# Gate logits with the gate's weights stationary, then turned back, in a post-layernorm attention and mixture-of-experts kernel

## The chip, the cores and the metric

The kernel runs on one core of one Trainium2 chip. The metric is the device time of one execution in microseconds (us). TensorE (PE in the profile) multiplies, ScalarE (ACT), VectorE (DVE) and GpSimd (POOL) do the rest of the arithmetic, and SyncE (SP) starts most of the transfers.

## What is computed

The reference is one transformer layer on x of shape (2, 2048, 256), all in fp32:

```
x = layernorm(x + attention(x))            # 16 heads of 16, rotary, causal
tokens = x.reshape(4096, 256)
logits = tokens @ gate_w.T                 # 8 experts
probs = softmax(logits); expert = argmax(probs)
rank = position of the token among its expert's tokens; kept if rank < 640
y = probs[expert] * (relu(token @ w1[expert] + b1) @ w2[expert] + b2)
x = layernorm(x + y)
```

The change touches the line with the logits alone.

## The kernel before, in words

The program has four stages, one after the other: `project_qkv`, `attention`, `project_and_gate` and `experts`. Each is a block in which every engine has its own instruction list, and the engines meet at semaphores. A stage ends when all its engines have ended, since the next takes over the memory.

`project_and_gate` (from L774) handles the 4096 tokens in eight chunks of 512; a chunk is four tiles of 128 tokens. On PE, the order is written out by hand in `both(n, ...)` (L994 to L1012), which holds the second half of chunk n and the gate of chunk n - 1:

- `turn_o` (L931, matmuls at L937) turns the attention output of a tile so that tokens lie on the partitions. DVE's `normalise` (L1100, L1102) divides by the softmax denominators.
- `turn_y` (L941, L947) turns the result back, ACT's `copy_yT` (L1039) copies it out of PSUM, and `project` (L952, L958) multiplies it by the output weights. DVE's `residual` (L1111, L1114, L1118) adds x and takes the statistics.
- `turn_x1` (L962, L966) turns a chunk's normalised rows (DVE's `norm_chunk`, L1123 to L1134) into psD, and ACT's `copy_x1T` (L1050) copies them to x1T: 256 channels in two halves (kt = 0, 1) on the partitions, 512 tokens along the free axis.
- `gate_logits` (L970, L976) multiplies x1T by the gate's weights: for each of four tiles and two halves, the 128 x 128 block of x1T is the stationary operand and the 8 columns of the weights are streamed. The result, 128 tokens x 8 experts for each tile, is in `logits`, a part of the bank psL.
- DVE's `choose` (L1154 to L1163) reads it: maximum, difference, one-hot choice. ACT's `exponentials` (L1054) needs the difference; PE's `rank_chunk` (L984 to L991) needs the one-hot; DVE's `place` (L1168 to L1190) needs both and gives each token its slot. POOL's `send` (L1245) scatters the rows to DRAM by the slots.

The order on DVE (`both`, L1192 to L1206) is fixed too: rest of normalise and residual 0 to 2 of chunk n, `choose(n - 1)`, residual 3, normalise 0 and 1 of chunk n + 1, `place(n - 1)`, `norm_chunk(n)`. ACT's (`both`, L1065 to L1074) is: copy_yT 0, two plain_rows (L1062, the rows with the second normalisation applied, stored to the output), copy_yT 1, two more, copy_yT 2, copy_x1T(n - 1), copy_yT 3, exponentials(n - 1), and `deviations(n)` with two square roots, L1043 and L1045. Exp and Sqrt need different function tables, so each chunk has two table loads.

After the eighth chunk the lists end with its gate alone: on PE `turn_x1`, `gate_logits`, `rank_chunk` (L1028 to L1030), on ACT `copy_x1T`, four `plain_rows`, `exponentials` (L1083 to L1085), on DVE `choose` and `place`, on POOL the last sends.

A matmul with fp32 operands stands in the trace as two records; a transpose as one. So L976 has 8 chunks x 4 tiles x 2 halves x 2 = 128 records.

Of the kernel before, what the change touches and what calls it, by code (L numbers as in the profile page):

```python
# [30 lines left out]
P = 128  # L31
B, T, C, H = 2, 2048, 256, 16
HS = C // H
KT = C // P
E, DFF = 8, 1024
CAP = math.ceil(1.25 * B * T / E)
CHUNK = 512
# [736 lines left out]
def project_and_gate(nc, x, o_d, wproj, bproj, gate, ident, before, ones, prefer, slot_base, tok0, slots_d, out_d,  # L774
# [4 lines left out]
    with ExitStack() as ctx:  # L779
        def sb(name, shape, dt=F32):  # L780
            return ctx.enter_context(nc.sbuf_tensor(name, shape, dt))
# [4 lines left out]
        def sem(name):  # L786
            return ctx.enter_context(nc.semaphore(name))
# [28 lines left out]
        rows = [sb(f"rows{i}", [P, TPC, RW]) for i in range(2)]  # L816
        plain = [sb(f"plain{i}", [P, TPC, C]) for i in range(2)]
        x1T = sb("x1T", [P, KT, CHUNK])
        top = sb("top", [P, TPC])
        shifted = sb("shifted", [P, TPC, E])  # L820
        wanted = sb("wanted", [P, TPC, E])
# [42 lines left out]
        plain_stored = [sem(f"plain_stored{i}") for i in range(2)]  # L864
        x1_turned = sem("x1_turned")
        x1T_ready = sem("x1T_ready")
        logits_ready = sem("logits_ready")
        gate_step = sem("gate_step")
        shifted_ready = sem("shifted_ready")
# [56 lines left out]
        @block.tensor  # L926
        def _(pe):
            pe.wait_ge(w_loaded, 16 * (n_w - 1))

            def turn_o(n, i, h, t):  # L930
                if t == 0:  # L931
                    pe.wait_ge(loaded[i], 32 * (h + 1))
                if not (isinstance(n, int) and n == 0 and t < 2):

                    pe.wait_ge(y_ready, 1 + TPC * n + t - 1)
                for g in range(NG):
                    last = nc.tensor.transpose(psA[t % 2][:, g * P:(g + 1) * P], o_s[i][:, g, t * P:(t + 1) * P],  # L937
                                               id_s[:])
                last.then_inc(o_turned, 1)

            def turn_y(n, t):  # L941
                m = TPC * n + t
                pe.wait_ge(y_ready, 1 + m + 1)

                pe.wait_ge(yT_ready, 1 + m)
                for kt in range(KT):
                    last = nc.tensor.transpose(psB[:, kt, :],  # L947
                                               y_s[t % 2][:].rearrange("p h d -> p (h d)")[:, kt * P:(kt + 1) * P],
                                               id_s[:])
                last.then_inc(y_turned, 1)  # L950

            def project(n, t):  # L952
                m = TPC * n + t
                pe.wait_ge(yT_ready, 1 + m + 1)

                pe.wait_ge(res_ready, 1 + m)
                for kt in range(KT):
                    last = nc.tensor.matmul(psC[t % 2][:, 0:C], yT[t % 2][:, kt, :], wproj_s[:, kt, :],  # L958
                                            start=(kt == 0), stop=(kt == KT - 1))
                last.then_inc(projected, 1)  # L960

            def turn_x1(n, i):  # L962
                pe.wait_ge(rows_ready, TPC * (n + 1))
                for kt in range(KT):
                    for t in range(TPC):
                        last = nc.tensor.transpose(psD[:, kt, t * P:(t + 1) * P],  # L966
                                                   rows[i][:, t, kt * P:(kt + 1) * P], id_s[:])
                last.then_inc(x1_turned, 1)

            def gate_logits(n):  # L970
                pe.wait_ge(x1T_ready, KT * (n + 1))

                pe.wait_ge(slots_ready, 1 + n)
                for t in range(TPC):
                    for kt in range(KT):
                        last = nc.tensor.matmul(logits[:, t, :], x1T[:, kt, t * P:(t + 1) * P], gate_s[:, kt, :],  # L976
                                                start=(kt == 0), stop=(kt == KT - 1))
                last.then_inc(logits_ready, 1)

            def rank_chunk(n):  # L980


                pe.wait_ge(onehot_ready, n + 1)
                nc.tensor.matmul(ranks[:], before_s[:], onehot[:], start=True, stop=False)  # L984
                for t in range(TPC - 1):
                    later = TPC - 1 - t
                    nc.tensor.matmul(ranks[:, t + 1:TPC, :], ones_s[:],
                                     onehot[:, t:t + 1, :].to_broadcast([P, later, E]),
                                     start=False, stop=(t == TPC - 2))
                for t in range(TPC):  # L990
                    last = nc.tensor.matmul(counts, ones_s[:], onehot[:, t, :], start=(t == 0), stop=(t == TPC - 1))  # L991
                last.then_inc(ranks_ready, 1)

            def both(n, i, h, h_next):  # L994


                turn_y(n, 0)
                turn_o(n, i, h, 2)
                turn_y(n, 1)
                project(n, 0)  # L1000
                turn_o(n, i, h, 3)
                turn_y(n, 2)
                project(n, 1)
                turn_x1(n - 1, 1 - i)
                turn_y(n, 3)
                project(n, 2)
                gate_logits(n - 1)
                project(n, 3)
                if h_next is not None:
                    turn_o(n + 1, 1 - i, h_next, 0)  # L1010
                    turn_o(n + 1, 1 - i, h_next, 1)
                rank_chunk(n - 1)  # L1012

            turn_o(0, 0, 0, 0)
            for t in range(TPC):
                if t + 1 < TPC:
                    turn_o(0, 0, 0, t + 1)
                turn_y(0, t)
                if t:
                    project(0, t - 1)  # L1020
            project(0, TPC - 1)
            turn_o(1, 1, 0, 0)
            turn_o(1, 1, 0, 1)
            for k in range(0, NC3 // 2 - 1):
                both(2 * k + 1, 1, k, k + 1)
                both(2 * k + 2, 0, k + 1, k + 1)
            both(NC3 - 1, 1, NC3 // 2 - 1, None)
            turn_x1(NC3 - 1, 1)  # L1028
            gate_logits(NC3 - 1)
            rank_chunk(NC3 - 1)  # L1030

        @block.scalar
        def _(act):
            act.wait_ge(w_loaded, 16 * (n_w - 1))
            act.wait_ge(set_up, 2)

            def copy_yT(n, t):
                act.wait_ge(y_turned, TPC * n + t + 1)
                nc.scalar.activation(yT[t % 2][:], psB[:], ACT.Copy).then_inc(yT_ready, 1)  # L1039

            def deviations(n, i):
                act.wait_ge(mv_ready, TPC * (n + 1))
                nc.scalar.activation(std[i][:], mv[i][:, :, 1], ACT.Sqrt, bias=eps_s[:]).then_inc(std_ready, 1)  # L1043
                act.wait_ge(var_step, 2 * (n + 1))
                nc.scalar.activation(std2[i][:], var2[i][:], ACT.Sqrt, bias=eps_s[:]).then_inc(std2_ready, 1)  # L1045

            def copy_x1T(n):
                act.wait_ge(x1_turned, n + 1)
                for kt in range(KT):
                    nc.scalar.activation(x1T[:, kt, :], psD[:, kt, :], ACT.Copy).then_inc(x1T_ready, 1)  # L1050

            def exponentials(n):
                act.wait_ge(shifted_ready, n + 1)
                nc.scalar.activation(expd[:], shifted[:], ACT.Exp).then_inc(exp_ready, 1)  # L1054

            def plain_rows(n, i, h, tiles):

                if tiles[0] == 0:
                    act.wait_ge(rstd2_ready, n + 1)
                    act.wait_ge(plain_stored[i], 1 + 16 * h)  # L1060
                for t in tiles:
                    nc.scalar.activation(plain[i][:, t, :], rows[i][:, t, 0:C], ACT.Copy,  # L1062
                                         scale=rstd2[i][:, t:t + 1]).then_inc(plain_ready, 1)

            def both(n, i, h_before):  # L1065
                copy_yT(n, 0)
                plain_rows(n - 1, 1 - i, h_before, (0, 1))
                copy_yT(n, 1)
                plain_rows(n - 1, 1 - i, h_before, (2, 3))
                copy_yT(n, 2)  # L1070
                copy_x1T(n - 1)
                copy_yT(n, 3)
                exponentials(n - 1)
                deviations(n, i)  # L1074

            for t in range(TPC):
                copy_yT(0, t)
            deviations(0, 0)
            for k in range(0, NC3 // 2 - 1):
                both(2 * k + 1, 1, k)  # L1080
                both(2 * k + 2, 0, k)
            both(NC3 - 1, 1, NC3 // 2 - 1)
            copy_x1T(NC3 - 1)  # L1083
            plain_rows(NC3 - 1, 1, NC3 // 2 - 1, range(TPC))
            exponentials(NC3 - 1)  # L1085

# [600 lines left out]
```

## Time and profile before

| what | us |
|---|---|
| median of 3 runs (lowest, highest) | 1468.92 (1464.8, 1473.62) |
| the profiled execution's own time | 1471.45 |
| its span, first to last instruction | 1469.4 |
| `project_and_gate` in the span, about | 1064 to 1205 |
| mean granted TensorE clock over the span | 0.928 |

Positions are microseconds from the start of the span. A busy time is that of an engine; idle time stands in square brackets in a timeline, with what ended it. A granted clock of 1.00 is 2.4 GHz and 0.50 is 1.2 GHz.

### The profile page before, as it was taken

Reading aid. Unit: us, or ns where it says so; the run is one execution under the profiler, and the core shown is the slowest. Engines: PE = TensorE matmul, PEld = TensorE weight load, DVE = VectorE, ACT = ScalarE, POOL = GpSimd, SP = SyncE. Lnnn points to the kernel's source line nnn. Section 1 sums busy time; section 2 is a strip of 40 time slices with the busy share of each in tenths; the row PEclk is TensorE's granted clock in tenths of the full one; section 3 lists DMA queues with packets and bytes.
Section 4 is the critical chain, followed back from the end, with each engine's and each line's share of the span. In section 5 each row is a group of like instructions: output and inputs, shape, how many; then the busy total and the mean of one; then the engine's idle time right before and its main releaser. Section 6 shows DMA issues by size and latency. Waiting matters only on the chain. (4 is left out here: it accounts for less than half of the span.)

```text
span 1469.4 us, 22852 instructions
## 1 busy us (share of the span) xinstructions
PE 1285.6 (87%) x7857; PEld 650.4 (44%) x7857; DVE 1197.5 (81%) x2812; ACT 798.6 (54%) x1130; POOL 277.3 (19%) x282
## 2 busy tenths in 40 slices
PE   6776379999999999999999999999577739999997
PEld 3433112333333333333333333332166638999997
DVE  5997679999999989999999999994067737888886
ACT  3443303666666666666666666667535434554542
POOL 3555430011010010110010110101233420211121
PEclk9888656999999999999999999999888859999998
DMA  4578454213113112121130130000346531334230
GB/s 147 162 213 255 144 123 74 67 35 87 31 30 87 31 53 63 31 82 35 50 96 26 35 88 9 8 16 9 109 135 196 170 106 66 122 98 152 94 98 24
DMA packets 119120, 126.90 MB, mean 86 GB/s; under 512 B 15452, under 2 KB 101599, under 8 KB 119008
## 3 DMA queue, kind: packets, MB, share of 16 engines
q1 hardware_dynamic: 115424, 117.00, 27.5%
q0 software_dynamic: 3584, 8.47, 1.6%
q8 instruction: 63, 1.03, 0.3%
q14 instruction: 49, 0.40, 0.1%
HBM read 83.02 MB, written 48.38 MB: 89 GB/s over the span
## 5 line engine op out<-in xcount | busy, mean ns | idle before, releaser
L656 ACT ACTIVATE probs<-scores 128x1024 f32<-128x1024 f32 (+3 forms) x640 | 539.0, 894 | 320.4 <-PE scores L549 319.6
L711 DVE TENSOR_REDUCE part_max<-ring 128x1 f32<-128x512 f32 x768 | 478.0, 683 | 24.7 <-PE ring L579 23.1
L579 PE MATMUL ring<-k_stack,q_stack 96*128 96x512 bf16 (+3 forms) x1280 | 406.6, 363 | 45.0 <-DMA k_stack<-pieces_d 30.0
L549 PE MATMUL scores<-q_stack,k_stack 99*128 99x512 bf16 (+3 forms) x1280 | 339.3, 349 | 2.4 <-ACT probs L656 1.6
L565 PE MATMUL out_p<-probs,v_s 128*32 128x512 f32 (+3 forms) x2560 | 299.8, 540 | 0.5 <-POOL probs L761 0.3
L579 PEld LDWEIGHTS ring<-k_stack,q_stack 96*128 96x128 bf16 x1280 | 114.9, 97 | 350.3 <-DVE part_max L711 147.7
L761 POOL TENSOR_SCALAR_AFFINE_SELECT probs<-probs 128x512 f32<-128x512 f32 x128 | 81.4, 636 | 773.4 <-ACT probs L656 773.4
L705 DVE CUSTOM_DVE_ANT_0 scratch<-ring,mask_s 128x384 f32<-128x384 f32 (+2 forms) x384 | 195.0, 550 | 17.2 <-issue 16.5
L549 PEld LDWEIGHTS scores<-q_stack,k_stack 99*128 99x128 bf16 x1280 | 112.8, 98 | 175.7 <-issue 65.2
L195 PE MATMUL psP<-xT,wqk_s 128*128 128x512 f32 x128 | 72.2, 728 | 35.4 <-ACT xT L234 30.9
L1425 PE MATMUL psY<-w_hi,h_hi 128*128 128x256 f32 x320 | 91.0, 284 | 0.0
L1427 PE MATMUL psY<-w_hi,h_lo 128*128 128x256 f32 x320 | 89.8, 281 | 0.0
L1426 PE MATMUL psY<-w_lo,h_hi 128*128 128x256 f32 x320 | 89.8, 281 | 0.0
L1459 ACT ACTIVATE h_whole<-psH,b_s 128x384 f32<-128x384 f32 (+1 forms) x128 | 66.9, 528 | 41.0 <-PE psH L1406 34.2
L565 PEld LDWEIGHTS out_p<-probs,v_s 128*32 128x32 f32 x2560 | 50.6, 107 | 87.3 <-issue 58.2
L1404 PE MATMUL psH<-x_hi,w_hi 128*128 128x384 f32 (+1 forms) x256 | 80.2, 313 | 7.9 <-issue 6.8
L1590 POOL DMA_INDIRECT out<-fin,token x40 | 44.6, 1114 | 212.8 <-DVE fin L1543 206.8
L1405 PE MATMUL psH<-x_lo,w_hi 128*128 128x384 f32 (+1 forms) x256 | 79.5, 311 | 0.0
L1406 PE MATMUL psH<-x_hi,w_lo 128*128 128x384 f32 (+1 forms) x256 | 79.4, 310 | 0.0
L195 PEld LDWEIGHTS psP<-xT,wqk_s 128*128 128x128 f32 x128 | 29.3, 235 | 74.7 <-issue 41.4
L1467 ACT ACTIVATE w_hi<-w_whole 128x1024 fp32r<-128x1024 f32 x32 | 33.5, 1057 | 51.8 <-DMA w_whole<-w 39.0
L1425 PEld LDWEIGHTS psY<-w_hi,h_hi 128*128 128x128 f32 x320 | 60.9, 190 | 0.0
(116 smaller groups left out, 1498.4 us busy)
## 6 DMA issues: line engine op xcount, KB each, us to landing
w_whole<-w SPq DMA_DIRECT2D x16, 1024.0 KB, 6.5
q_stack<-pieces_d SPq DMA_DIRECT2D x192, 64.0 KB, 2.9
k_stack<-pieces_d SPq DMA_DIRECT2D x192, 64.0 KB, 2.9
v_d<-vt SPq DMA_DIRECT2D x8, 1024.0 KB, 4.4
v_s<-v_d SPq DMA_DIRECT2D x8, 1024.0 KB, 6.1
o_d<-o_s SPq DMA_DIRECT2D x32, 256.0 KB, 2.2
p_o<-o_d SPq DMA_DIRECT2D x8, 1024.0 KB, 6.1
slots_d<-no_row SPq DMA_DIRECT2D x1, 5200.0 KB, 30.0
```

Source lines behind the costliest of these rows:

```text
L195: last = nc.tensor.matmul(psP[:, g, :], wqk_s[:, kt, g * P:(g + 1) * P], xT[i][:, kt, :], start=(kt == 0), stop=(kt == KT - 1))
L549: last = nc.tensor.matmul(scores[p][:, hh, off:CHUNK], k_stack[i][0:KROWS, kb // TPC, j, kb % TPC * P:(kb % TPC + 1) * P], q_stack[i][0:KR ...
L565: last = nc.tensor.matmul(out_p[j * VW:(j + 1) * VW, off:CHUNK], v_s[i][:, kb, j * VW:(j + 1) * VW], probs[n % NPROB][:, j, off:CHUNK], st ...
L579: last = nc.tensor.matmul(slot[:, h * w:(h + 1) * w], q_stack[i][0:SROWS, qt // TPC, j + h, qt % TPC * P:(qt % TPC + 1) * P], k_stack[i][0 ...
L656: nc.scalar.activation(probs[n % NPROB][:, 2 * p:2 * p + 2, off:CHUNK], scores[p][:, :, off:CHUNK], ACT.Exp, scale=SCALE).then_inc(exp_don ...
L705: nc.vector.tensor_tensor_reduce(out=scratch[:, j, 0:w], in0=ring[m % 3][:, 0:w], in1=mask_s[:, CHUNK - w:CHUNK], scale=1.0, scalar=LOWEST ...
L711: nc.vector.tensor_reduce(part_max[:, qt, j, t:t + 1], ring[m % 3][:, 0:w], axis=AX.X, op=ALU.max).then_inc(ring_read, 1)
L761: nc.gpsimd.affine_select(out=block_, in_=block_, compare_op=ALU.is_ge, fill=0.0, base=0, pattern=[[0, HPU], [1, P]], channel_multiplier=- ...
L1404: nc.tensor.matmul(out, w_hi[i][0][:, kt, cols], hi, start=(kt == 0), stop=False)
L1425: nc.tensor.matmul(out, h_hi[:, ft, slots], w_hi[i][1][:, ft, :], start=(ft == 0), stop=False)
L1426: nc.tensor.matmul(out, h_hi[:, ft, slots], w_lo[i][1][:, ft, :], start=False, stop=False)
L1427: last = nc.tensor.matmul(out, h_lo[:, ft, slots], w_hi[i][1][:, ft, :], start=False, stop=(ft == FT - 1))
```

## The change

The product is formed the other way round: `gate_logits` now streams the 512 tokens of x1T against the gate's 8 columns as the stationary operand, one matmul for each half, into 8 partitions of psD (free, since x1T was copied out of it). ACT copies the 8 x 512 result to a new tile, `gated_s`, in `copy_gated`. A new function on PE, `turn_logits`, turns it tile by tile into the old place in psL. On PE `turn_logits(n - 1)` stands after `project(n, 3)`; on ACT `copy_gated(n - 1)` stands after the fourth copy_yT and ahead of the exponentials. After the eighth chunk `copy_gated` stands ahead of the four plain_rows. The wait for `slots_ready` moves to `turn_logits`. DVE, POOL and SP are as before.

```diff
             def gate_logits(n):
                 pe.wait_ge(x1T_ready, KT * (n + 1))
+                for kt in range(KT):
+                    last = nc.tensor.matmul(psD[0:E, 0, :], gate_s[:, kt, :], x1T[:, kt, :],
+                                            start=(kt == 0), stop=(kt == KT - 1))
+                last.then_inc(gated, 1)
+
+            def turn_logits(n):
+                pe.wait_ge(gated_copied, n + 1)
 
                 pe.wait_ge(slots_ready, 1 + n)
                 for t in range(TPC):
-                    for kt in range(KT):
-                        last = nc.tensor.matmul(logits[:, t, :], x1T[:, kt, t * P:(t + 1) * P], gate_s[:, kt, :],
-                                                start=(kt == 0), stop=(kt == KT - 1))
+                    last = nc.tensor.transpose(logits[:, t, :], gated_s[:, t * P:(t + 1) * P], id_s[0:E, 0:E])
                 last.then_inc(logits_ready, 1)
...
                 gate_logits(n - 1)
                 project(n, 3)
+                turn_logits(n - 1)
...
             gate_logits(NC3 - 1)
+            turn_logits(NC3 - 1)
             rank_chunk(NC3 - 1)
...
+            def copy_gated(n):
+                act.wait_ge(gated, n + 1)
+                nc.scalar.activation(gated_s[:], psD[0:E, 0, :], ACT.Copy).then_inc(gated_copied, 1)
...
                 copy_yT(n, 3)
+                copy_gated(n - 1)
                 exponentials(n - 1)
...
             copy_x1T(NC3 - 1)
+            copy_gated(NC3 - 1)
             plain_rows(NC3 - 1, 1, NC3 // 2 - 1, range(TPC))
             exponentials(NC3 - 1)
```

## Rows read from the trace of the kernel before

**Rows 1.** Busy time by engine in the stage `project_and_gate`.
```profile
1064.00:1205.00 141.00, 97.62 (x576) 82.42 (x576) 87.25 (x368) 59.26 (x120) 50.36 (x40) 0.78 0.46 150
```
**Rows 2.** Timeline of a middle chunk: start us, us, engine, line, operation [idle before].
```profile
1101.43 1.08 ACT L1050 ACTIVATE x1T<-psD 128x512 f32<-128x512 f32 x2 [1.60 <-PE psD L966]
1102.57 1.95 PE L976 MATMUL psL<-gate_s,x1T 128*128 128x8 f32 x16 [0.18 <-ACT x1T L1050]
1102.81 1.28 ACT L1054 ACT_TABLE_LOAD   x1
1104.37 1.11 PE L958 MATMUL psC<-wproj_s,yT 128*128 128x256 f32 x4
1104.55 0.19 DVE L1154 TENSOR_REDUCE top<-psL 128x4 f32<-128x32 f32 x1 [0.96 <-PE psL L976]
1105.00 0.23 ACT L1054 ACTIVATE expd<-shifted 128x32 f32<-128x32 f32 x1 [0.91 <-DVE shifted L1156]
1105.32 1.04 PE L937 MATMUL psA<-p_id,p_o 128*128 128x128 f32 x8
1106.75 0.30 ACT L1043 ACTIVATE std<-mv,eps_s 128x4 f32<-128x4 f32 x1 [0.22 <-DVE mv L1118]
1109.33 0.18 DVE L1123 RECIPROCAL rstd<-std 128x4 f32<-128x4 f32 x1
1109.93 0.30 ACT L1045 ACTIVATE std<-var,eps_s 128x4 f32<-128x4 f32 x1 [2.88 <-DVE var L1128]
1110.14 0.36 ACT L1039 ACTIVATE yT<-psB 128x256 f32<-128x256 f32 x1
1110.65 0.66 PE L947 MATMUL psB<-p_id,y_s 128*128 128x128 f32 x2 [2.40 <-ACT yT L1039]
1118.43 1.95 PE L976 MATMUL psL<-gate_s,x1T 128*128 128x8 f32 x16
```
**Rows 3.** Last 2.4 us before each of PE's seven restarts: stretch, PE busy, clock, DMA.
```profile
1077.84:1080.24 2.40, 0.00 (x0) 0.76 0.00 0
1093.55:1095.95 2.40, 0.01 (x1) 1.00 0.00 0
1108.25:1110.65 2.40, 0.00 (x1) 0.83 0.01 3
1124.11:1126.51 2.40, 0.01 (x1) 1.00 0.00 0
1138.72:1141.12 2.40, 0.00 (x1) 0.88 0.00 0
1153.29:1155.69 2.40, 0.00 (x1) 0.69 1.05 360
1168.83:1171.23 2.40, 0.01 (x2) 1.00 0.00 0
```
**Rows 4.** The same view from restart to gate, second and third time.
```profile
1096.00:1102.60 6.60, 6.42 (x31) 0.74 0.46 137
1110.70:1118.40 7.70, 7.64 (x30) 0.61 0.55 145
```
**Rows 5.** Timeline after the eighth chunk.
```profile
1188.31 1.69 ACT L1062 ACTIVATE plain<-rows,rstd 128x256 f32<-128x256 f32 x4
1188.47 3.58 PE L976 MATMUL psL<-gate_s,x1T 128*128 128x8 f32 x16 [1.17 <-ACT x1T L1050]
1192.09 0.19 DVE L1154 TENSOR_REDUCE top<-psL 128x4 f32<-128x32 f32 x1 [6.73 <-PE psL L976]
1193.32 0.18 DVE L1170 TENSOR_REDUCE total<-expd 128x4 f32<-128x32 f32 x1
1195.67 0.97 POOL L1245 DMA_INDIRECT slots_d<-rows,slot_index  x1 [6.68 <-DVE slot_index L1190]
```
**Rows 6.** 512-column fp32 products of the first stage: timeline, then one line's durations.
```profile
55.92 3.60 PE L195 MATMUL psP<-xT,wqk_s 128*128 128x512 f32 x8
L195 PE MATMUL psP<-xT,wqk_s x128: 592/592/1222, 12.3 to 158.2; 128*128 128x512 f32 x128
```

More of the change, by code:

```diff
@@ L818, in project_and_gate @@
         x1T = sb("x1T", [P, KT, CHUNK])
+        gated_s = sb("gated_s", [E, CHUNK])
         top = sb("top", [P, TPC])
@@ L866, in project_and_gate @@
         x1T_ready = sem("x1T_ready")
+        gated = sem("gated")
+        gated_copied = sem("gated_copied")
         logits_ready = sem("logits_ready")
```

## The prediction

> **What bounds the kernel now.** First the busy times of the stage that the change touches [rows 1]: of 141 us PE works 97.62, DVE 87.25, ACT 59.26, POOL 50.36, at a mean clock of 0.78. No engine fills the stage, so it runs on a loop of hand-overs, and the timeline of one chunk shows which. I read it from one gate to the next [rows 2]. G is the start of the gate's products, 1102.57. They end at G+1.95; DVE, which had been idle for 0.96, starts `choose` at G+1.98 and from there works without a gap through residual 3, two normalises and `place` to `norm_chunk` (G+6.76) and its two small products. ACT's second square root waited 2.88 for them (G+7.36), and the copy of yT queued behind it starts at G+7.57. PE was idle for 2.40 until that copy and restarts at G+8.08. From the restart to the next gate, at 1118.43, PE is busy nearly all the time (7.64 of 7.70 us) [rows 4]. So a chunk is one stretch bound by PE and, after the gate, one bound by DVE's list, and **the moment at which the logits reach DVE starts the second**. Anything added between the two is paid in full, in each of the seven rounds.
>
> The second thing is the clock. Before each of the seven restarts it is at or on the way to the low level: over the last 2.4 us its mean was 0.76, 1.00, 0.83, 1.00, 0.88, 0.69 and 1.00 [rows 3]. Where it was below 0.85 it had fallen 0.8 to 1.5 us before the restart, and the low clock then lasted long; where it fell later, the burst was shorter (mean clock 0.74 in a burst of 6.6 us against 0.61 in one of 7.7) [rows 4]. The ends of rows 3 are the restarts, so their differences are the periods: 15.71, 15.86 and 15.54 after an early fall, 14.70, 14.61 and 14.57 after a late one. Mean 15.70 against 14.63: a **long burst costs 1.07 us more than a short one**.
>
> **The change, part by part.**
> *Products.* Removed: 16 records in 1.95 us (a pace of 0.113 behind a last one of 0.256). Added: 2 matmuls, 4 records of 512 columns. The first stage has such records: 8 in 3.60, the last 0.592, so a pace of (3.60 - 0.592)/7 = 0.43 [rows 6]. Here they end at G + 3 x 0.43 + 0.592 = G+1.88, and the next product can start at about G+1.76. So the sixteen cost what the four cost, within 0.1 us: the saving in count buys nothing. That row has 128 stationary columns, not 8. Fewer might drain sooner: 0.3 less at the lower end (nothing in 1.88 is shorter than its four paces of 0.43); the upper end is the row.
>
> *Copy on ACT.* The nearest row is x1T's, 128 x 512 in two of 1.08 together, 0.594 each; it began about 0.13 behind PE, and PE began 0.06 behind its end [rows 2]. I take 0.13 + 0.59 + 0.06: the copy ends at G+2.60 and PE may read at G+2.66. The lower bound is the 0.23 of the exponential on 32 columns; the row on 512 columns is also the upper, as partitions are fewer. ACT has nothing else to do there: copy_yT 3 is done, and what was behind it was the table load for Exp, which ran at G+0.24 under the gate's products. That load now comes behind the copy, from G+2.60 to 3.88.
>
> *Project 3* starts at G+1.76 and not G+1.80, so the copy is hidden behind it: four records later, by the row 0.95 after its start (1104.37 to 1105.32), PE is at G+2.71. Copy and product end together, with 0.05 of slack. If the product weren't there, the copy would cost its 0.78.
>
> *Four turns.* PE's turns of 128 columns go 8 in 1.04, so a pace of 0.11 and 0.27 for the last [rows 2]. Four: 3 x 0.11 + 0.27 = 0.60, taken, though these stream only 8 columns: before, 16 records with 8 streamed columns and 128 stationary ones had the same pace of 0.113. Bounds: 0.3 (no pace between them but the last's 0.27) to 1.1 (four of 0.27 unpipelined). The logits are there at G+3.31 and DVE starts at G+3.33 instead of G+1.98: **1.35 us later**.
>
> *Behind it on PE* come the eight turns of `turn_o` and `rank_chunk`. They move by 0.5, less than DVE's 1.35, and so still wait for the one-hot or not at all. *Behind it on ACT:* the exponential's input now comes at about G+3.8, its table at 3.88, so 0.1 late and for nobody, as `place` reads it 3 us later; then Sqrt's table until 5.4, while the statistics come at G+4.18 + 1.35 = 5.53. Free, if the covers hold; 0.2 us is the margin. POOL and SP issue what they issued, 1.35 later, with their waits unchanged in kind.
>
> Sum over seven rounds: 7 x 1.35 = **9.45 us**.
>
> *Clock.* The second restart, 1095.95, had the fall just after it (clock 1.00 up to it). It now comes 1.35 later, while nothing before it has moved, so the fall lies ahead of it as for the first and third: a long burst. From it the next period is 15.71 + 1.35 = 17.06, and I take it that the fall keeps its place in such a chunk, so that all stay long. Four of the seven bursts were short (second, fourth, fifth, seventh): 4 x 1.07 = **4.3 us**. Lower bound: none of them changes, or one or two of the long ones turn short (-2); upper bound: this 4.3.
>
> *After the eighth chunk* the clock is at the low level: 16 products take 3.58 and the stage waits on this chain [rows 5]. With C = 1188.47: four products at half the clock, 3 x 0.86 + 1.06 to 1.22 = C+3.7; copy to C+4.4. The four plain_rows, which ran under the products, now stand behind the copy: C+4.4 to C+6.1. Then Exp's table load, C+7.4, the exponential, C+7.6. Logits turned at about C+5.6; `choose` is done by C+6.7, so the exponential is what `place` waits for. `total` starts at C+7.6 = 1196.0 instead of 1193.32, and the last sends with it: **2.7 us**. Here ACT's order costs more than PE's work does. Bounds: 1.9 (the turned logits alone) and 3.2 (colder turns and the full record).
>
> The sum: 9.45 + 4.3 + 2.7 = 16.4 us. The profiled execution took 1471.45 (span 1469.4), which gives 1487.9; it lies 2.5 above the median, so against the median of 1468.92 the forecast is **1485**.
>
> **A rule against the trace.** In rows 2 a table load takes 1.28 us, and ACT's first square root ran 0.22 behind the statistics it needs, 1.5 us after the exponential began. The Trainium skill (ScalarE: Activation LUTs, What ACT_TABLE_LOAD costs) adds about 1.38 us of draining to each load, 2.66 in all. The row is against it.
>
> **The rivals.**
> *A. The clock keeps its mix* of long and short bursts, by other phases: 9.45 + 2.7 = 12.2, or 1481. For it: in the rows the kinds alternate without a simple order. Against: the second restart is moved the wrong way.
> *B. Table loads become the bound.* Both now stand behind the copy. If each held ACT for twice its 1.28 us, Exp's would end at G+5.2 and Sqrt's at G+8.0; std would be ready at G+8.3, against DVE's need at 6.76 + 1.35 = G+8.1. That adds 0.2 to 0.3 a round, 2 us in all, and 1.3 in the tail: 1488. For it only the small margin; against it the 0.22 above. The rule of the Trainium skill named above would bring this about.
> *C. The clock stays up, and the kernel isn't slower.* The gate would stream 4 x 512 columns where it streamed 16 x 8, right ahead of PE's pause. If that kept the clock at the high level through the restart, each burst would give back half its low time: (1 - 0.74) x 6.6 = 1.7 in a short and (1 - 0.61) x 7.7 = 3.0 in a long one, 4 x 1.7 + 3 x 3.0 = 15.8 [rows 4]. Against 12.2 that is -3.6: 1465. It needs six of the seven bursts to break even. Against it: the clock falls 5 us and more behind the gate, after a pause of 2.4 that the change doesn't shorten.
> *D. The change does less than it says*: products with 8 stationary columns cost half of the row. Then the copy ends at G+1.7 and the turns at G+2.5, 0.5 a round, and about 1 in the tail: +4.5, 1473.
>
> **How the numbers follow.** Forecast (delay and long bursts) 0.50; A 0.27; B 0.03; C 0.05; D 0.07; 0.08 for what I don't see (mostly a delay of 1.7 by slower turns or copy: 7 x 0.35 = 2.5 more, 1488). 0.5% is 7.3 us and about what a measurement of this kernel can tell from no change, as its three runs lie 8.8 apart. Slower by more: forecast, A, B and most of the rest, 0.86. Within: D, most of C, 0.12. Faster by more: 0.02. Range: the low end takes A with its lower bounds (a delay of 1.0: 7.0 + 1.9 = 9 us, 1478) and a median that may fall 3 lower; the high end the forecast with the delay of 1.7 and 3 of scatter: 1475 to 1491.
>
> **What the profile would show.** Right: from the first gate record to DVE's `top` 3.3 us instead of 1.98, with PE's turns as the releaser; PE's pause before its restart still about 2.4 by yT; seven restarts with periods near 17.1 and a clock below 0.85 ahead of each; at the end `total` released by ACT's exponential, 2.7 later in the tail. Wrong: `top` within 2.5 us (D), periods of 15.9 and clock 1.00 before restarts (A), a wait of DVE's L1123 for ACT (B), or a clock of 1.00 through the bursts (C).

## The result, and the profile after

| what | before | after |
|---|---|---|
| median of the runs on one chip (4 each), us | 1470.63 | 1485.57 |
| lowest, highest | 1464.8, 1473.62 | 1485.21, 1488.32 |
| the profiled execution, its span | 1471.45, 1469.4 | 1485.21, 1483.1 |
| ratio of the runs, 95% interval | | 1.0107 [1.008, 1.0135] |

The change makes the kernel slower by 14.9 us between the medians. The forecast was 1485 and +16.4 us. At 1% it is small, but the interval of the ratio lies clear of 1. The line numbers of after are higher by 3 to 8 on PE's part, 10 to 14 on ACT's and 16 on DVE's.

First the busy times of the stage, which answer to [rows 1]; the columns are the same.

```profile
1064.00:1218.00 154.00, 103.48 (x512) 71.02 (x512) 87.30 (x368) 63.86 (x128) 50.49 (x40) 0.79 0.42 138
```

DVE does the same work (87.30 against 87.25 us) in a stage 13 us longer. PE has 64 records fewer and its weight loads 11.4 us less (71.02 against 82.42), yet 5.9 more of matmul: a count of instructions that falls while the time grows. The gate itself is busy for 19.9 us (L976 and the turns at L985) where it had 17.2, and of the rounds from the first gate to the seventh more runs at the low clock (mean 0.83 against 0.85). The timeline of one round says what happened, line by line against [rows 2].

```profile
1103.02 1.88 PE L976 MATMUL psD<-x1T,gate_s 128*8 128x512 f32 x4
1104.83 1.13 PE L961 MATMUL psC<-wproj_s,yT 128*128 128x256 f32 x4
1104.94 0.59 ACT L1064 ACTIVATE gated_s<-psD 8x512 f32<-8x512 f32 x1 [1.70 <-PE psD L976]
1105.54 1.28 ACT L1068 ACT_TABLE_LOAD   x1
1105.89 0.41 PE L985 MATMUL psL<-p_id,gated_s 8*128 8x8 f32 x4
1106.34 0.19 DVE L1170 TENSOR_REDUCE top<-psL 128x4 f32<-128x32 f32 x1 [2.20 <-PE psL L985]
1106.83 0.23 ACT L1068 ACTIVATE expd<-shifted 128x32 f32<-128x32 f32 x1
1108.55 0.30 ACT L1053 ACTIVATE std<-mv,eps_s 128x4 f32<-128x4 f32 x1 [0.18 <-DVE mv L1134]
1111.73 0.30 ACT L1055 ACTIVATE std<-var,eps_s 128x4 f32<-128x4 f32 x1 [2.89 <-DVE var L1144]
1112.45 0.41 PE L950 MATMUL psB<-p_id,y_s 128*128 128x128 f32 x2 [2.40 <-ACT yT L1049]
```

With G = 1103.02 the four products end at G+1.88, the copy at G+2.51, the turns at G+3.28, and DVE starts at **G+3.32** where it started at G+1.98. Everything behind has moved by 1.34 or 1.35: the second square root from G+7.36 to G+8.71, PE's restart from G+8.08 to G+9.43. PE's pause ahead of it is 2.40 as before. ACT's first root still waits for the statistics, 0.18, so the table load behind the copy is covered.

Next, the last 2.4 us before PE's restarts, which answer to [rows 3]: stretch, PE busy, clock, DMA.

```profile
1079.93:1082.33 2.40, 0.09 (x2) 1.00 0.24 49
1094.35:1096.75 2.40, 0.00 (x1) 0.90 0.00 0
1110.05:1112.45 2.40, 0.00 (x1) 1.00 0.00 0
1126.00:1128.40 2.40, 0.00 (x1) 0.70 0.00 0
1142.91:1145.31 2.40, 0.01 (x1) 0.74 0.00 0
1159.90:1162.30 2.40, 0.00 (x1) 0.75 1.08 361
1176.92:1179.32 2.40, 0.00 (x1) 0.76 0.00 0
```

The first of these rows stands at another place of the list than the others: it is the turn of a chunk's third tile and not of its second (the last section says why). From the fourth restart on, the clock has fallen early each time, and the periods (from the ends of these rows: 14.42, 15.70, 15.95, 16.91, 16.99, 17.02) settle near 17.0. Those of 15.70 and 15.95 are still of the short kind, the 14.63 of before and the delay. Last, the eighth chunk's end, as in [rows 5].

```profile
1199.02 3.38 PE L976 MATMUL psD<-x1T,gate_s 128*8 128x512 f32 x4 [1.17 <-ACT x1T L1060]
1202.44 0.59 ACT L1064 ACTIVATE gated_s<-psD 8x512 f32<-8x512 f32 x1 [3.47 <-PE psD L976]
1202.93 1.69 ACT L1076 ACTIVATE plain<-rows,rstd 128x256 f32<-128x256 f32 x4
1204.64 1.28 ACT L1068 ACT_TABLE_LOAD   x1
1206.19 0.18 DVE L1186 TENSOR_REDUCE total<-expd 128x4 f32<-128x32 f32 x1 [1.35 <-ACT expd L1068]
```

From the first gate record to `total` 7.17 us passed, against 4.85, and what `total` waited for is ACT's exponential.

Where the time went, between the two profiled executions: the first gate came 0.54 earlier (1087.33 against 1087.87); the six rounds from there to the seventh gate took 99.61 against 89.87, 9.74 more, of which 6 x 1.34 = 8.0 is delay and the other 1.7 is put down to the clock, as four of the six rounds are now of the long kind where two were (2 x 1.07 = 2.1); the way to the eighth gate 12.08 against 10.73 (1.35); the tail 2.32. Sum 12.87, which is just how much later the last `total` is. The last stage took 1.0 more, which nothing in the change touches. These are single executions: two more kernels below have the same loop as the changed one, and their six rounds took 100.32 and 100.12, so that 2.2 to 2.4 is left beside the delay and not 1.7.

### The profile page after: what moved, and what is told of

The parts are those of the page before. It is cut to its first block and busy times, and to the rows that moved or that the text cites. A ratio compares the mean times of both kernels' runs of the same rounds, so it can differ in the third digit from the quotient of the medians.

```text
span 1483.1 us, 22732 instructions
## 1 busy us (share of the span) xinstructions
PE 1291.3 (87%) x7793; PEld 638.8 (43%) x7793; DVE 1197.9 (81%) x2812; ACT 803.2 (54%) x1138; POOL 278.1 (19%) x282
## 5 line engine op out<-in xcount | busy, mean ns | idle before, releaser
L705 DVE CUSTOM_DVE_ANT_0 scratch<-ring,mask_s 128x384 f32<-128x384 f32 (+2 forms) x384 | 195.0, 550 | 17.2 <-issue 16.5
```

The lines of the kernel that those rows point to most:

```text
L705: nc.vector.tensor_tensor_reduce(out=scratch[:, j, 0:w], in0=ring[m % 3][:, 0:w], in1=mask_s[:, CHUNK - w:CHUNK], scale=1.0, scalar=LOWEST ...
```

## The experiments

"Before" beside each ratio is the kernel before, run on the same chip in the same session. Gate to gate is the time between the first gate records of two chunks.

### Move the gate only

```diff
-                gate_logits(n - 1)
                 project(n, 3)
+                gate_logits(n - 1)
```

> The kernel before with one line moved: the sixteen small gate products stand behind project 3, their form unchanged, no copy and no turns. My theory (what counts is when the logits reach DVE, whatever forms them): project 3 needs 0.95 us and waits some 0.2 for its yT, so DVE's first gate instruction comes about 3.2 us after the end of project 2 instead of 1.98, nearly the changed kernel's 3.32. Each of seven rounds is 1.1 to 1.3 us longer and most bursts after a restart are long ones: 8 us from the delay, 1 to 4 from the clock, nothing in the tail, so 1479.5 to 1483. Rival 1 (the new form costs by itself, by its copy on ScalarE and its turns): a mere reordering costs nothing, within 2 us of before. Rival 2 (the loss is mainly in the tail): within 2 us of before as well.

Measured: 1482.03, ratio 1.0077 [1.0065, 1.009]. A middle round, DVE and PE around the gate:

```profile
1100.14 1.08 ACT L1050 ACTIVATE x1T<-psD 128x512 f32<-128x512 f32 x2 [2.10 <-PE psD L966]
1101.79 1.10 PE L958 MATMUL psC<-wproj_s,yT 128*128 128x256 f32 x4 [0.61 <-DVE res L1111]
1102.73 1.85 PE L976 MATMUL psL<-gate_s,x1T 128*128 128x8 f32 x16
1104.62 0.19 DVE L1154 TENSOR_REDUCE top<-psL 128x4 f32<-128x32 f32 x1 [2.22 <-PE psL L976]
```

Without a copy, a turn or a wide product, DVE starts 3.40 us behind the end of x1T's copy (1101.22 to 1104.62). Before it was 2.04 (1102.51 to 1104.55), in the changed kernel about 3.4. The gates came 16.75, 16.91, 16.98, 17.03, 17.04, 17.06 apart. So the same delay, made by an order of instructions alone, gives the same rounds as the change. Both rivals fall: they had it within 2 us of before, and it is 11.3 above. No cost of the new form by itself shows in the loop; what it costs is the time at which its last piece lands.

### The change in the loop only

The eighth chunk's gate is formed as before, the seven in the loop as after.

```diff
+            def gate_tail(n):
+                pe.wait_ge(x1T_ready, KT * (n + 1))
+                pe.wait_ge(slots_ready, 1 + n)
+                for t in range(TPC):
+                    for kt in range(KT):
+                        last = nc.tensor.matmul(logits[:, t, :], x1T[:, kt, t * P:(t + 1) * P], gate_s[:, kt, :],
+                                                start=(kt == 0), stop=(kt == KT - 1))
+                last.then_inc(logits_ready, 1)
...
-            gate_logits(NC3 - 1)
-            turn_logits(NC3 - 1)
+            gate_tail(NC3 - 1)
             rank_chunk(NC3 - 1)
...
             copy_x1T(NC3 - 1)
-            copy_gated(NC3 - 1)
             plain_rows(NC3 - 1, 1, NC3 // 2 - 1, range(TPC))
```

> The changed kernel, but the eighth chunk's gate, behind the loop, in the old form (sixteen products, no copy_gated ahead of the plain_rows). Theory: only the tail's term comes back: from the last gate's first record to DVE's total 4.85 us instead of 7.17, so 2.3 us below the changed kernel, about 1483; the seven rounds keep periods of up to 17.0. Rival (the loss is in the tail's order on ScalarE, and the loop's share is small): 8 us or more come back, at most 1477.

Measured: 1484.63, ratio 1.01 [1.0085, 1.0115]. From the last gate's first record (1198.44) to `total` (1203.29) it is 4.85 us again, and the rounds stay with periods up to 17.03. The rival, 1477 or less, falls. The median doesn't show the whole 2.3 us: the last stage took 266.6 us here and 265.0 in the profiled execution after, so a term of 2 us has to be read in the trace.

### Filler products in PE's pauses, before and after

The same products, which compute nothing that is used, in both kernels.

```diff
+            def filler(k):
+                for _ in range(k):
+                    nc.tensor.matmul(psC[0][:, C:2 * C], wproj_s[:, 0, 0:P], wproj_s[:, 1, :], start=True, stop=True)
...
+                filler(1)
                 turn_y(n, 0)
                 turn_o(n, i, h, 2)
+                filler(4)
                 turn_y(n, 1)
```

> The kernel before with filler products on PE (256 columns into a part of psC[0] that nobody reads): one ahead of turn_y 0, four ahead of turn_y 1, in PE's pauses of 0.84 and 2.40 us. The products compute nothing that is used. It prices the clock alone. Theory: at the high clock a filler is 0.43 us, the five fit into the pauses, the clock stays at 1.00 through the restarts, and the low time in the seven bursts is given back: 4 x 1.7 + 3 x 3.0 = 15.8 us by the rows of before, so 1455 to 1459. Rival 1 (the clock falls anyway, since the fillers don't keep it up): the four take 3.4 us at half the clock and overrun the pause by 1 us, so 5 to 8 us slower than before. Rival 2 (the clock is not on the path of the rounds): within 2 us of before.

> The changed kernel with the same filler products in the same places. Theory: with the clock held high on both sides, what is left between this one and the kernel before with fillers is the delay of the logits and the tail alone: 7 x 1.34 + 2.3 = 11.7 us; and it lies about 14 to 16 us below the changed kernel, so 1469 to 1472. Rival 1 (the delay matters only by way of the clock): the two kernels with fillers lie within 4 us of each other. Rival 2 (the clock has no part in the loss): this one lies 14.9 above the other with fillers, as without them.

Measured: 1462.51 on the kernel before, ratio 0.9943 [0.9931, 0.9956], and 1471.29 on the changed one, ratio 1.0008 [0.9999, 1.0016]. A window of about a round, first of the one on before, then of the other; the clock is the number behind the brackets.

```profile
1110.00:1124.00 14.00, 12.49 (x87) 1.00 0.63 192
```
```profile
1113.00:1128.00 15.00, 12.84 (x75) 1.00 0.57 177
```

The clock stays at 2.4 GHz through the restarts, and every round becomes alike: gates 13.57 apart in the first kernel, 14.90 in the second. **The difference, 1.33 us, is the delay without the clock**, as read from the timeline (1.34). The rival by which the delay counts only through the clock is refuted, and so is that of fillers that do not hold it up.

On the changed kernel the fillers give back about 14 us (1471.29 against 1485.57, two sessions with nearly the same before), as expected. Two sizes were off. The clock gave back 8.2 us on the kernel before, not 12 to 16, so that its 1462.51 lies outside the expected 1455 to 1459. The timeline of a round shows why: at the high clock PE runs into ACT, whose first two plain_rows wait for DVE's `rstd` and stand ahead of the second yT copy, and so of the third tile's turn.

```profile
1107.05 0.41 PE L947 MATMUL psB<-p_id,y_s 128*128 128x128 f32 x2 [0.67 <-ACT yT L1045]
1107.88 0.91 ACT L1068 ACTIVATE plain<-rows,rstd 128x256 f32<-128x256 f32 x2 [0.98 <-DVE rstd L1145]
1108.69 0.36 ACT L1045 ACTIVATE yT<-psB 128x256 f32<-128x256 f32 x1
1109.20 0.41 PE L947 MATMUL psB<-p_id,y_s 128*128 128x128 f32 x2 [0.44 <-ACT yT L1045]
1112.52 1.95 PE L976 MATMUL psL<-gate_s,x1T 128*128 128x8 f32 x16
```

From restart to gate it is 5.47 us where before had 6.62 (second round, 1095.95 to 1102.57) and 7.78 (third): 1.15 less than the short kind, and I had taken 1.7. Half the low time isn't what the clock costs; what counts is the part of it in which PE is what the others wait for. Second, the medians of the two kernels with fillers lie 8.8 apart and not 11.7. In the profiled executions the last `total` is 12.98 later (1195.38 against 1182.40): 1.12 from the first gate, 8.0 from six rounds, 1.34, and 2.52 in the tail. The last stage then took 267.1 us in the first and 263.7 in the second. That stage is the same program in all kernels here and differs by up to 3.4 us between these executions; the cause of that stays open. So the clock's share in the loss isn't settled by the medians: 14.9 less 8.8 is 6.1 us, where the rounds of the traces have about 2, and the last stage's 3.4 makes up most of the gap.

### The tail's order on ScalarE

```diff
-            copy_gated(NC3 - 1)
             plain_rows(NC3 - 1, 1, NC3 // 2 - 1, range(TPC))
+            copy_gated(NC3 - 1)
```

> The changed kernel with one line moved on ScalarE: behind the loop, copy_gated stands behind the four plain_rows, which then run under the last gate's products. Theory (ScalarE's order, not PE's work, sets the tail): from the last gate's first record to DVE's total 7.17 us become 5.8, limited by the turned logits and choose; 1.4 us less in the trace, the median within its scatter of the changed kernel's (1484 or so). Rival (the products and turns set the tail): no change of the 7.17.

Measured: 1483.57, ratio 1.0091 [1.0074, 1.0108]. From the first record of the last gate, 1198.26, to `total`, 1203.98, it is 5.72 us, against 7.17. Here are ACT's lines of the tail:

```profile
1198.09 1.70 ACT L1076 ACTIVATE plain<-rows,rstd 128x256 f32<-128x256 f32 x4
1201.66 0.59 ACT L1064 ACTIVATE gated_s<-psD 8x512 f32<-8x512 f32 x1 [1.88 <-PE psD L976]
1202.27 1.28 ACT L1068 ACT_TABLE_LOAD   x1
1203.56 0.23 ACT L1068 ACTIVATE expd<-shifted 128x32 f32<-128x32 f32 x1
```

The four plain_rows, 1.70 us of work for nobody in a hurry, now run under the products. Of the tail's 2.3 us, 1.45 were this one line's place and 0.9 the new form. The medians can't show it: this ratio's interval overlaps that of the changed kernel.

### The turns ahead of project 3

```diff
                 gate_logits(n - 1)
-                project(n, 3)
                 turn_logits(n - 1)
+                project(n, 3)
```

> The changed kernel with turn_logits ahead of project 3, so that PE stands still for the copy. Theory: the logits reach DVE at G+3.1 instead of G+3.32, and as project 3 isn't needed before DVE has chosen (about G+4.2), the round gets shorter by the 0.2 and no longer by PE's pause: 1.5 us less in all, about 1484; the periods, at 17.0 by the clock, may hardly move. Rival (project 3 as a cover is worth its 0.78, since PE's work is on the path): the round gets longer by 0.5, 3 us in all, 1489.

Measured: 1482.48, ratio 1.008 [1.0066, 1.0095].

```profile
1102.45 1.88 PE L976 MATMUL psD<-x1T,gate_s 128*8 128x512 f32 x4
1105.01 0.41 PE L985 MATMUL psL<-p_id,gated_s 8*128 8x8 f32 x4 [0.68 <-ACT gated_s L1064]
1105.45 0.19 DVE L1170 TENSOR_REDUCE top<-psL 128x4 f32<-128x32 f32 x1 [1.89 <-PE psL L985]
```

DVE starts at G+3.00, and PE's idle 0.68 under the copy costs nothing. The gates came 15.69, 16.75, 16.91, 16.98, 15.61 and 15.69 apart: never more than the changed kernel's longest, three of them of the short kind and 0.3 shorter than the changed kernel's 15.95. So the cover that the change gave the copy was worth less than the 0.32 us that it kept DVE waiting; the rival, 1489, falls. (Whether the median itself is lower than the changed kernel's is not shown, as the intervals overlap.) Even so DVE starts 1 us later than before: 1.88 of products, 0.7 of copy with its hand-overs, 0.4 of turns, against 1.95 in one piece.

### The second root later on ScalarE, before and after

```diff
-                act.wait_ge(var_step, 2 * (n + 1))
-                nc.scalar.activation(std2[i][:], var2[i][:], ACT.Sqrt, bias=eps_s[:]).then_inc(std2_ready, 1)
+            def second_root(n, i):
+                act.wait_ge(var_step, 2 * (n + 1))
+                nc.scalar.activation(std2[i][:], var2[i][:], ACT.Sqrt, bias=eps_s[:]).then_inc(std2_ready, 1)
...
                 copy_yT(n, 0)
+                second_root(n - 1, 1 - i)
                 plain_rows(n - 1, 1 - i, h_before, (0, 1))
```

> The kernel before with the second square root of deviations(n) moved behind the first copy_yT of chunk n + 1 on ScalarE, so that this copy, and PE behind it, no longer wait for DVE's list. Theory: the pause of 2.40 splits; PE turns the second tile and projects the first while DVE is in its list, and then waits for normalise 2 behind DVE's norm_plain: 1.5 us less a round, 8 to 12 in all, 1459 to 1463. Rival (DVE's stretch is the loop whatever ScalarE does, as norm_plain needs the root): within 3 us of before.

> The same move in the changed kernel. Theory: DVE's stretch from the logits is still in the chain, so the delay of 1.33 a round and 2.3 in the tail stay: 9 to 14 above the other kernel with this move. Rival (the delay was paid only since the restart hung on the root): within 5 us of it.

Measured: 1461.47 on the kernel before, ratio **0.994 [0.9927, 0.9952]**, which beats both kernels; 1478.86 on the changed one, ratio 1.0064 [1.0051, 1.0077]. The first one's timeline shows that the second tile's turn (1106.37) no longer pauses; the pause stands one tile later and is 2.69 long. Its window shows the clock.

```profile
1105.84 0.38 ACT L1039 ACTIVATE yT<-psB 128x256 f32<-128x256 f32 x1 [0.80 <-PE psB L947]
1106.37 0.41 PE L947 MATMUL psB<-p_id,y_s 128*128 128x128 f32 x2
1107.93 0.30 ACT L1047 ACTIVATE std<-var,eps_s 128x4 f32<-128x4 f32 x1 [1.71 <-DVE var L1132]
1109.48 0.91 ACT L1064 ACTIVATE plain<-rows,rstd 128x256 f32<-128x256 f32 x2 [1.25 <-DVE rstd L1143]
1110.29 0.36 ACT L1039 ACTIVATE yT<-psB 128x256 f32<-128x256 f32 x1
1110.80 0.41 PE L947 MATMUL psB<-p_id,y_s 128*128 128x128 f32 x2 [2.69 <-ACT yT L1039]
```
```profile
1109.00:1123.00 14.00, 9.79 (x72) 1.00 0.57 192
```

So PE's restart did hang on a root that it doesn't need. But the expectation named what comes next wrongly: PE then waits for the second yT copy, behind plain_rows that wait for `rstd`, and not for a normalise. The gates come 13.57 apart, with the clock at 1.00 in the middle rounds, and that is to 0.01 the round of the kernel with fillers, whose root stands in its old place. **At the high clock the root's place changes nothing in the round**: in both, the third tile's turn comes 8.26 behind `top` (1100.94 to 1109.20, 1102.54 to 1110.80), by way of DVE's list and the plain_rows. What the move gives is that the clock stays up: between its two pauses PE now works from 1105.37 to 1108.11, where it had worked from 1107.38 to 1108.25, and the clock doesn't fall. In the changed kernel the gates come 14.91 apart where the clock stays up, again 1.34 more, and 16.41 to 16.58 where it falls:

```profile
1098.00:1113.00 15.00, 10.56 (x65) 1.00 0.55 182
1113.00:1128.00 15.00, 13.51 (x64) 0.77 0.42 150
```

So the two medians lie 17.4 apart, beyond my 9 to 14. In the profiled executions the last `total` is 15.9 later: 0.8 from the first gate, 11.4 from six rounds, 1.3, and 2.3 in the tail. Here the delay costs more than its 8.0 in the rounds, since three of the six fall to the low clock where the other kernel has at most the first. The rival (within 5 us) falls.

## Why the prediction was right

*The number.* The forecast of 1485 was met by 1485.57, and part of that is luck. The sum was 16.4; in the profiled executions the last `total` is 12.9 later, and the medians lie 14.9 apart, while the median of before moved from 1468.92 to 1470.63 with its fourth run. Of the three terms the delay came out as summed, the clock and the tail smaller.

*What bounds the kernel.* Right: the moment of the logits starts the stretch bound by DVE, and the delay is paid in full in each round. It is shown three ways: by the shifted timeline, by the moved gate, and by rounds of 13.57 and 14.90 at a steady clock.

*The sum of one round.* 3.33 was forecast and 3.32 measured, from two errors that cancel. The turns took 0.41 and not 0.60: their matmuls last 0.20 each and follow each other at 0.07. And they began at G+2.87 and not at G+2.71, 1.06 behind project 3's start instead of 0.95. Products (1.88) and copy (0.59) were as the rows of other shapes had them: neither 8 stationary columns in place of 128 nor 8 partitions in place of 128 made them shorter. (The forecast's lower bound for the products, 0.3 less, doesn't follow from its own paces: 1.88 less four of 0.43 is 0.16.)

*The covers.* All held: DVE never waited for ACT's first root, and the exponential came at its table load's end. Rival B is refuted by the 0.18 that the root waited for its statistics. (The prediction says that in the kernel before this root began 1.5 us after the exponential began; the rows have 1.75, and 1.52 is from the exponential's end. As the load needs 1.28 of it, the argument stands.) Exp's load began at 1105.54 and lasted 1.28, and the exponential began at 1106.83, at once. The 1.38 us of draining that the Trainium skill adds (ScalarE: Activation LUTs, What ACT_TABLE_LOAD costs) is not there.

*The clock.* Mechanism right, size off: 4.3 us forecast, 1.7 in the rounds, or 1.2 with the earlier first gate. The step that failed is "nothing before it has moved". The first restart itself had moved, as told below, and the second and third burst were short ones. The fourth and later periods, 16.91 to 17.02, come near the 17.06 that the prediction worked out. The change is not what moved the first restart, as the last section shows. Nor does that move alone make the short bursts: in the two other kernels with this loop, whose first chunk runs alike, no round was short (16.02 and 15.93 for the first, both at a mean clock of 0.79, against 15.69 at 0.89). What sets the clock's fall against the first pauses differs from one execution to the next and stays open; the forecast read its short and long bursts from one. In the kernel with the moved gate all rounds but the first lie at 16.9 to 17.1. Rival A (1481) was thus nearer for the first rounds and the forecast for the last.

*The tail.* 2.7 forecast, 2.3 measured: the clock rose within the last gate, so that the products took 3.38 and not 3.7 and the turns 0.41. That ACT's order weighs more than PE's work is shown by the moved line, 1.45 of 2.32.

*Rivals C and D* did not happen: the clock fell as before, and products of 8 stationary columns cost what the row of the first stage said.

## What to carry to other kernels

Fewer instructions on an engine are worth nothing where they take the same time, and a result that has to pass another engine before it can be used is late by that pass; ask when its last piece lands, and who starts then. When a wait is traced to an engine's list, look for what stands at the head of that list and whether it is needed there: one line's place (the second root behind the first copy) gave 9.7 us, two thirds of what the rewritten product lost. Then ask why it helped: here not by a shorter chain, as the rounds of 13.57 are there with the root in either place once the clock stays up, but with PE's longer work between its pauses, through which the clock stayed up. And read a delay on a path that pauses PE with the clock in mind: the same 1.33 us a round cost 8.0 us in six rounds with the clock held up, and 11.4 where it toppled rounds into the low clock.

## What the runs showed that I had not expected

*Some of VectorE's instructions are held while GpSimd adds.* In the first chunk, one DVE instruction on 128 x 4 elements took 2.15 us, where its median is 0.16. Before, the three lines around it:

```profile
1076.94 2.34 POOL L1237 TENSOR_TENSOR xb<-p_x,bproj_s 128x1024 f32<-128x1024 f32 x1 [6.87 <-DMA p_x<-x]
1077.15 2.15 DVE L1126 TENSOR_TENSOR var<-mv,rstd 128x4 f32<-128x4 f32 x1
1079.53 0.30 ACT L1045 ACTIVATE std<-var,eps_s 128x4 f32<-128x4 f32 x1 [3.38 <-DVE var L1128]
```

It ended with POOL's addition (1079.28). In the changed kernel the addition came at 1078.35, and what was long is the four-part normalisation, which takes 1.4 to 1.6 us elsewhere:

```profile
1077.48 3.41 DVE L1150 TENSOR_SCALAR rows<-res,mv,rstd 128x256 f32<-128x256 f32 x4
1077.60 0.30 ACT L1055 ACTIVATE std<-var,eps_s 128x4 f32<-128x4 f32 x1 [1.41 <-DVE var L1144]
1078.35 2.39 POOL L1253 TENSOR_TENSOR xb<-p_x,bproj_s 128x1024 f32<-128x1024 f32 x1 [8.02 <-DMA p_x<-x]
```

There the root and yT are no longer late, and the first long pause falls at the third tile. This has nothing to do with the gate: in seven of the eight experiments, of both forms, it is again the normalisation that is held (3.4 to 3.5 us) and in the eighth, the moved gate, nothing is, as it had all but ended when the addition began. The kernel before's is the one execution with L1126 held. Nor is everything on DVE held. In later chunks DVE adds the residual from PSUM (0.42) and takes its statistics (0.43) during an addition in their usual time.

The Trainium skill (GPSIMD Engine Reference, Specifications) has the SBUF interfaces shared with VectorE, with contention for its instructions that have two SBUF inputs or run in a 2-port mode. L1126 has two SBUF inputs, and the rows agree, with DVE held until the other's instruction ends. The normalisation reads one tensor from SBUF beside a mean and a factor for each partition, and no row tells which of the two cases it is. What set the addition's place, the landing of x, was not varied.

*The clock rose in some last gates and not in others.* In the tail PE had been on the low clock. Sixteen products of 8 columns kept it busy from 1188.47 to 1192.05 in the kernel before, and the clock stayed at 0.50; four of 512 columns, from 1199.02 to 1202.40 in the changed one, and it rose. First a window of before, then two of after:

```profile
1190.40:1192.40 2.00, 1.65 (x8) 0.50 0.65 242
```
```profile
1199.00:1201.00 2.00, 1.98 (x3) 0.50 0.32 104
1202.00:1204.00 2.00, 0.81 (x5) 0.98 0.01 2
```

The form doesn't settle it. None of the five executions with the old form in the tail shows a rise, and four of the five with the new form do. The fifth, the changed kernel with fillers, ran the same four products after the same instructions, and the clock stayed at 0.50 through them and through the turns behind them, which took 0.59 where they take 0.41 at the high clock:

```profile
1188.01 3.58 PE L976 MATMUL psD<-x1T,gate_s 128*8 128x512 f32 x4 [1.17 <-ACT x1T L1066]
```

So its tail took 7.37 us and not 7.17. It counted only there. What decides between a rise and none is not shown.
